# The sine half of a rotary embedding on GpSimd: two instructions of 1024 columns become four of 512

## Chip, core and metric

The kernel runs on one core of a Trainium2 chip. The metric is the device time of one execution in microseconds (us). All data are float32.

## What is computed

The reference applies one full-attention block to x (8 sequences of 512 tokens, 128 features), then six layers of windowed attention (16 heads of 64, window 32) with a gated feed-forward part, and adds both back to x. The change lies in the windowed attention, where q and k are normalised per head and then rotated:

```python
q = l2norm(q) * qs                       # (k likewise)
cos, sin = (jnp.cos(freqs), jnp.sin(freqs))
q = q * cos * scale + rotate_half(q) * sin * scale
k = k * cos * inv + rotate_half(k) * sin * inv
```

`rotate_half` swaps the two halves (32 values each) of every head and negates one of them; the sign is in the sine table.

## The kernel before

After a prologue (the full-attention block, some 290 us) the six layers run as one stream of 192 tiles n = 0..191 of 128 tokens: 6 layers, 8 sequences, 4 tiles (j = n % 4) each. The four tiles of one sequence in one layer are called a batch. Each engine has its own list of steps per tile, written out by hand in `slot(c)`, one list for each of the four values of c % 4, in which steps of several tiles are mixed (`step(c, lag, ...)` runs tile c - lag). Engines meet only through semaphores.

The steps that matter here:

- VectorE (DVE), in this order in each slot: `sumsq` of the new tile for q (L1364), `sums` of the softmax of an older tile (L1332), its reciprocal (L1337), `sumsq` for k (L1364), `probs` (L1342: Pr times rs, both in SBUF), `probs_back` (L1357, a transposition), `cos_part` of the tile before (L1378: raw times the cosine table, both in SBUF, 2048 columns), `rotated` (L1384: rot plus swp, both in SBUF), in the fourth slot `ffn_stats` (L1390, L1395), `maxes` (L1320), `less_max` (L1325), and last `normed` of the new tile (L1370: raw times rr, both in SBUF).
- GpSimd (POOL): `norms` (L1100, a maximum on 32 columns into ssm, and L1102, the power -1/2 into rr, which `normed` needs), then `sin_part` (L1112, which needs `normed` and writes swp for `rotated`). Between them lie, by slot, steps of the feed-forward part: `gated` (L1128, three in a batch), `ffn_y` (L1133), `x_between` (L1121), `ffn_rstd` (L1139, L1141).
- GpSimd's order over a batch is: norms(0), sin(0); norms(1), gated 1, sin(1), gated 0; gated 2, norms(2), ffn_y, sin(2), x_between; norms(3), ffn_rstd, sin(3). So `sin_part` of a tile is followed by norms of the next tile at once for j = 3 and j = 0, by two `gated` steps for j = 1, and by `x_between` for j = 2.
- ScalarE copies projections out of PSUM (L875, which waits for `rotated` of the tile before the last), squares them (L883), and makes the normed rows of the feed-forward part (L959, which waits for `ffn_rstd`); TensorE transposes rot (L571), and `cos_part` waits for such a transposition because it overwrites rot.

Of the kernel before, what the change touches and what calls it, by code (L numbers as in the profile page):

```python
# [7 lines left out]
ALU = mybir.AluOpType  # L8
# [6 lines left out]
HEADS, DH, W = 16, 64, 32  # L15
INNER = HEADS * DH
HID = int(D * 4 * 2 / 3)
P = 128
# [42 lines left out]
def wait(eng, sem, value):  # L61

    if type(value) is int and value <= 0:
        return
    eng.wait_ge(sem, value)


def adaln_block(nc, x_d, wq_d, wk_d, wv_d, wo_d, bq_d, bk_d, bv_d, bo_d, cT_d, wmod_d,
# [3 lines left out]
    with ctx:  # L72
        def sb(name, shape, dt=F32):
            return ctx.enter_context(nc.sbuf_tensor(name, shape, dt))
# [13 lines left out]
        TS = sb("TS", [P, DEPTH, TPB, 2, DH])  # L88
# [223 lines left out]
        def layer(n):  # L312
            return n // NT
# [741 lines left out]
        def _(pool):  # L1055
# [48 lines left out]
            def sin_part(n, b, j):  # L1104

                pool.wait_ge(qn_ready, n + 1)
                wait(pool, rot_ready, n)
                src = raw[:, j % 2, :].rearrange("p (i h t d) -> p i h t d", i=2, t=2, d=32)
                dst = swp[:, :].rearrange("p (i h t d) -> p i h t d", i=2, t=2, d=32)
                for t in range(2):  # L1110
                    tab = TS[:, layer(n), j, :, 32 * t:32 * t + 32]
                    last = pool.tensor_tensor(dst[:, :, :, t, :], src[:, :, :, 1 - t, :],  # L1112
                                              tab.unsqueeze(2).broadcast_to([P, 2, HEADS, 32]), ALU.mult)
                last.then_inc(sin_ready, 1)

            def x_between(b):
# [26 lines left out]
            def slot(c):  # L1143
                if c % TPB == 0:
                    step(c, 0, norms)
                    step(c, 0, sin_part)
                elif c % TPB == 1:
                    step(c, 0, norms)
                    batch(c, 2, gated, 1)
                    step(c, 0, sin_part)  # L1150
                    batch(c, 2, gated, 0)
                elif c % TPB == 2:
                    batch(c, 2, gated, 2)
                    step(c, 0, norms)
                    batch(c, 2, ffn_y)
                    step(c, 0, sin_part)
                    batch(c, 1, x_between)
                else:
                    step(c, 0, norms)
                    batch(c, 1, ffn_rstd)  # L1160
                    step(c, 0, sin_part)
# [322 lines left out]
```

## Time and profile before

| | |
|---|---|
| Median of 3 runs | 3816.96 us (3797.87 to 3832.17) |
| The profiled execution: its own time | 3803.09 us |
| Its span, first to last instruction | 3801.2 us |
| Mean granted TensorE clock | 0.96 |
| Busy: PE, DVE, ACT, POOL | 89%, 87%, 64%, 72% |

Busy shares are of the span. Spans are recorded by engine; a busy engine may be held up inside an instruction, and then the instruction is recorded as longer.

### The profile page before, as it was taken

What the parts mean: (1) busy time and instruction counts of PE and PEld (TensorE: products, weight loads), DVE (VectorE), ACT (ScalarE), POOL (GpSimd) and SP (SyncE); (2) the same over time, 40 slices, a digit from 0 to 9 for tenths busy, and PEclk for the clock granted to TensorE, in tenths of its full rate; (3) what the DMA queues carried; (4) which work ended last, traced back from release to release, by engine and by line L of the source; (5) the groups of instructions that cost most, each with busy time, mean ns of one, the idle gap of its engine ahead of it and who ended that gap; (6) DMA issues with size and microseconds to landing.
All of it is one profiled execution on the core that took longest, in us unless ns stands there. A gap on an engine that the chain in (4) does not pass through costs nothing.

```text
span 3801.2 us, 108012 instructions
## 1 busy us (share of the span) xinstructions
PE 3394.8 (89%) x46108; PEld 2202.2 (58%) x46108; DVE 3304.5 (87%) x2938; ACT 2421.1 (64%) x3929; POOL 2746.2 (72%) x1233
## 2 busy tenths in 40 slices
PE   4666899999999999999999999999999998999987
PEld 2333566666666665665665666665666665666654
DVE  4667899998899998899998999998999998998982
ACT  2444666666666666666766766666666666666764
POOL 3006787777787877777777787877777787787781
PEclk8778999999999999999999999999999999999997
DMA  2000111111111111111111111111111111111111
GB/s 69 3 1 14 34 38 34 38 45 45 38 39 34 38 45 44 39 38 33 34 50 44 41 36 34 39 45 44 44 34 37 34 45 46 42 34 37 35 32 40
DMA packets 132142, 141.98 MB, mean 37 GB/s; under 512 B 37580, under 2 KB 75856, under 8 KB 131664
## 3 DMA queue, kind: packets, MB, share of 16 engines
q1 hardware_dynamic: 131664, 135.09, 14.4%
q8 instruction: 364, 5.96, 0.7%
q14 instruction: 114, 0.93, 0.1%
HBM read 19.62 MB, written 2.10 MB: 6 GB/s over the span
## 4 chain that ended last, share of the span: by engine, by line
PE 37%; DVE 24%; POOL 13%; issue 11%; ACT 3%; SPq 3%; DMA 2%; POOLq 0%; ACTq 0%; DVEq 0%
PE bank L562 11%; POOL rr L1102 6%; PE mid L612 5%; DVE Pr L1342 4%; DVE raw L1370 4%; PE mid L571 4%; PE bank L660 4%; DVE rot L1378 4%; PE bank L631 4%; POOL swp L1112 3%; PE mid L599 3%; PE mid L619 2%; DVE rot L1384 2%; PE bank L668 2%; DVE ss L1364 2%
## 5 line engine op out<-in xcount | busy, mean ns | idle before, releaser
L1112 POOL TENSOR_TENSOR swp<-raw,TS 128x1024 f32<-128x1024 f32 x384 | 899.8, 2371 | 616.3 <-DVE raw L1370 616.3
L1102 POOL TENSOR_TENSOR rr<-ssm,nhalf 128x32 f32<-128x32 f32 x192 | 1213.3, 6319 | 16.0
L562 PE MATMUL bank<-wqkv,xs 128*128 128x512 f32 x2304 | 1203.5, 625 | 22.6 <-DMA xs<-F 8.5
L875 ACT ACTIVATE raw<-bank 128x512 f32<-128x512 f32 x768 | 434.3, 591 | 549.2 <-DVE rot L1384 503.3
L571 PEld LDWEIGHTS mid<-ident,rot 128*128 128x128 f32 x3072 | 365.9, 143 | 388.0 <-issue 333.6
L571 PE MATMUL mid<-ident,rot 128*128 128x128 f32 x3072 | 442.0, 277 | 136.5 <-DVE rot L1384 131.6
L562 PEld LDWEIGHTS bank<-wqkv,xs 128*128 128x128 f32 x2304 | 385.4, 192 | 289.9 <-issue 192.2
L1364 DVE TENSOR_REDUCE ss<-sq 128x16 f32<-128x1024 f32 x384 | 463.3, 1207 | 95.4 <-ACT sq L883 94.8
L1370 DVE TENSOR_TENSOR raw<-raw,rr 128x2048 f32<-128x2048 f32 x192 | 469.2, 2444 | 35.5 <-POOL rr L1102 35.5
L1378 DVE TENSOR_TENSOR rot<-raw,TC 128x2048 f32<-128x2048 f32 x192 | 440.4, 2294 | 41.7 <-PE mid L571 40.5
L1384 DVE TENSOR_TENSOR rot<-rot,swp 128x2048 f32<-128x2048 f32 x192 | 440.1, 2292 | 20.7 <-DVE rot L1378 0.9
L612 PEld LDWEIGHTS mid<-PT,V 128*64 128x64 f32 x6144 | 340.0, 138 | 191.4 <-issue 165.6
L883 ACT ACTIVATE sq<-raw 128x1024 f32<-128x1024 f32 x384 | 407.0, 1060 | 31.3 <-DVE ss L1364 25.0
L612 PE MATMUL mid<-PT,V 128*64 128x128 f32 x6144 | 383.9, 278 | 37.1 <-DMA PT<-PTd 32.8
L631 PE MATMUL bank<-OT,fwo 128*128 128x128 f32 x3072 | 383.1, 279 | 1.4 <-ACT OT L922 1.4
L631 PEld LDWEIGHTS bank<-OT,fwo 128*128 128x128 f32 x3072 | 367.6, 196 | 2.0 <-issue 2.0
L1342 DVE TENSOR_TENSOR Pr<-Pr,rs 128x1024 f32<-128x1024 f32 x192 | 359.0, 1870 | 0.1
L599 PEld LDWEIGHTS mid<-kT,qT 64*32 64x32 f32 x24576 | 273.7, 105 | 87.1 <-issue 82.5
L660 PE MATMUL bank<-xn,w 128*128 128x512 f32 (+1 forms) x576 | 313.5, 626 | 7.2 <-ACT ge L972 3.8
L599 PE MATMUL mid<-kT,qT 64*32 64x64 f32 x24576 | 309.5, 225 | 0.8 <-issue 0.8
L900 ACT ACTIVATE qT<-mid 128x512 f32<-128x512 f32 x384 | 230.1, 599 | 91.9 <-PE mid L571 88.2
L1332 DVE TENSOR_REDUCE sm<-Pr 128x16 f32<-128x1024 f32 x192 | 232.6, 1211 | 49.9 <-ACT Pr L916 49.9
(132 smaller groups left out, 4325.4 us busy)
## 6 DMA issues: line engine op xcount, KB each, us to landing
PT<-PTd SPq DMA_DIRECT2D x1344, 64.0 KB
xs<-F SPq DMA_DIRECT2D x192, 64.0 KB, 1.9
BT<-PTd SPq DMA_DIRECT2D x192, 64.0 KB
wqkv<-d_wqkv SPq DMA_DIRECT2D x36, 256.0 KB, 2.7
fwo<-d_fwo SPq DMA_DIRECT2D x6, 512.0 KB, 4.0
d_out<-X SPq DMA_DIRECT2D x8, 256.0 KB, 2.3
w<-d_w SPq DMA_DIRECT2D x6, 341.0 KB
w<-d_w SPq DMA_DIRECT2D x6, 128.0 KB
```

The costliest lines, as they stand in the source:

```text
L562: nc.tensor.matmul(bank[bk][:, :], xs[:, j, :], wqkv[:, c, :], start=True, stop=True)\
L571: mm = nc.tensor.transpose(bank[QK_BANK[i]][:, u * P:(u + 1) * P], rot[:, col:col + P], ident[:, :])
L599: mm = nc.tensor.matmul(bank[3 + h][w * W:(w + 1) * W, u * DH:(u + 1) * DH], qT[r, j % 2, u, w * W:(w + 1) * W], kT[r, u, j * P + w * W:j ...
L612: mm = nc.tensor.matmul(OUT_BANK[u // 4][h * DH:(h + 1) * DH, (u % 4) * P:(u % 4 + 1) * P], V[:, j % 2, hc:hc + DH], PT[:, :, h * HH + u, ...
L631: mm = nc.tensor.matmul(bank[6][:, j * P:(j + 1) * P], fwo[:, c, :], OT[:, c, :], start=(c == 0), stop=(c == HH - 1), skip_group_check=True)
L1102: pool.tensor_tensor(rr[:, :], ssm[:, :], nhalf[:, :], ALU.pow).then_inc(rr_ready, 1)
L1112: last = pool.tensor_tensor(dst[:, :, :, t, :], src[:, :, :, 1 - t, :], tab.unsqueeze(2).broadcast_to([P, 2, HEADS, 32]), ALU.mult)
L1342: nc.vector.tensor_tensor(pr, pr, rs[:, :].unsqueeze(2).broadcast_to([P, HEADS, DH]), ALU.mult)\
L1364: nc.vector.tensor_reduce(ss[:, s], sq[:, :].rearrange("p (h d) -> p h d", d=DH), AX.X, ALU.add).then_inc(ss_ready[i], 1)
L1370: nc.vector.tensor_tensor(q, q, rr[:, :].unsqueeze(2).broadcast_to([P, 2 * HEADS, DH]), ALU.mult)\
L1378: nc.vector.tensor_tensor(rot[:, :].rearrange("p (i h d) -> p i h d", i=2, d=DH), q, tab.unsqueeze(2).broadcast_to([P, 2, HEADS, DH]), ALU ...
L1384: nc.vector.tensor_tensor(rot[:, :], rot[:, :], swp[:, :], ALU.add).then_inc(rot_ready, 1)
```

## The change

`sin_part` runs once per tile. Before, it issued one instruction for each half t of the heads, over q and k together (2 x 16 x 32 = 1024 columns). Now the loop over q and k (i) is outside, so that there are four instructions of 16 x 32 = 512 columns. The data, the waits before the first, the signal after the last and the place in GpSimd's order are the same.

```diff
-                for t in range(2):
-                    tab = TS[:, layer(n), j, :, 32 * t:32 * t + 32]
-                    last = pool.tensor_tensor(dst[:, :, :, t, :], src[:, :, :, 1 - t, :],
-                                              tab.unsqueeze(2).broadcast_to([P, 2, HEADS, 32]), ALU.mult)
+                for i in range(2):
+                    for t in range(2):
+                        tab = TS[:, layer(n), j, i:i + 1, 32 * t:32 * t + 32]
+                        last = pool.tensor_tensor(dst[:, i, :, t, :], src[:, i, :, 1 - t, :],
+                                                  tab.broadcast_to([P, HEADS, 32]), ALU.mult)
                 last.then_inc(sin_ready, 1)
```

## Rows read from the trace of the kernel before

**Rows 1.** The page: span, part 1, and the chain's shares by engine

```profile
span 3801.2 us, 108012 instructions
PE 3394.8 (89%) x46108; PEld 2202.2 (58%) x46108; DVE 3304.5 (87%) x2938; ACT 2421.1 (64%) x3929; POOL 2746.2 (72%) x1233
PE 37%; DVE 24%; POOL 13%; issue 11%; ACT 3%; SPq 3%; DMA 2%; POOLq 0%; ACTq 0%; DVEq 0%
```

**Rows 2.** DVE's waits (us in total, times, longest), and one line's durations (ns min/median/max)

```profile
DVE raw L1370 <- POOL rr L1102: 35.5, 15, 6.1
...
L1342 DVE TENSOR_TENSOR Pr<-Pr,rs x192: 1214/1892/2336, 342.4 to 3734.5; 128x1024 f32<-128x1024 f32 x192
```

**Rows 3.** Durations of GpSimd multiplications of 1024 and of 64 columns

```profile
L1112 POOL TENSOR_TENSOR swp<-raw,TS x384: 2322/2367/3348, 305.2 to 3703.3; 128x1024 f32<-128x1024 f32 x192
...
L1067 POOL TENSOR_TENSOR TS<-xn,qks x24: 315/315/318, 12.6 to 34.9; 128x64 f32<-128x64 f32 x24
```

**Rows 4.** Timeline, tile 191 (start, us, engine, line; brackets: idle before)

```profile
3701.02 5.65 POOL L1112 TENSOR_TENSOR swp<-raw,TS 128x1024 f32<-128x1024 f32 x2 [1.50 <-DVE raw L1370]
...
3702.39 2.06 DVE L1342 TENSOR_TENSOR Pr<-Pr,rs 128x1024 f32<-128x1024 f32 x1
```

**Rows 5.** Timeline, POOL and DVE, from normed(106) to normed(107), j = 2

```profile
2190.79 3.04 DVE L1370 TENSOR_TENSOR raw<-raw,rr 128x2048 f32<-128x2048 f32 x1
...
2193.91 4.69 POOL L1112 TENSOR_TENSOR swp<-raw,TS 128x1024 f32<-128x1024 f32 x2 [2.23 <-DVE raw L1370]
...
2197.37 2.31 DVE L1342 TENSOR_TENSOR Pr<-Pr,rs 128x1024 f32<-128x1024 f32 x1
...
2198.87 1.77 POOL L1121 TENSOR_TENSOR FX<-qks,F 128x513 f32<-128x513 f32 x1 [0.26 <-ACT qks L931]
...
2200.61 0.29 POOL L1100 TENSOR_SCALAR ssm<-ss 128x32 f32<-128x32 f32 x1
...
2200.89 2.25 DVE L1378 TENSOR_TENSOR rot<-raw,TC 128x2048 f32<-128x2048 f32 x1
...
2209.03 2.28 DVE L1370 TENSOR_TENSOR raw<-raw,rr 128x2048 f32<-128x2048 f32 x1
```

**Rows 6.** The same stretch of another batch, normed(98) to normed(99), and after

```profile
2057.47 2.25 DVE L1378 TENSOR_TENSOR rot<-raw,TC 128x2048 f32<-128x2048 f32 x1
2057.49 2.38 POOL L1100 TENSOR_SCALAR ssm<-ss 128x32 f32<-128x32 f32 x1
...
2059.82 2.29 DVE L1384 TENSOR_TENSOR rot<-rot,swp 128x2048 f32<-128x2048 f32 x1
2059.96 7.47 POOL L1102 TENSOR_TENSOR rr<-ssm,nhalf 128x32 f32<-128x32 f32 x1
...
2067.46 2.29 DVE L1370 TENSOR_TENSOR raw<-raw,rr 128x2048 f32<-128x2048 f32 x1 [1.76 <-POOL rr L1102]
...
2071.00 1.14 ACT L959 ACTIVATE xn<-bank,rstd 128x128 f32<-128x128 f32 x4 [3.87 <-POOL rstd L1141]
```

**Rows 7.** Timeline, normed of tiles 97, 101 and 105 (j = 1)

```profile
2028.65 2.28 DVE L1370 TENSOR_TENSOR raw<-raw,rr 128x2048 f32<-128x2048 f32 x1
...
2102.65 2.28 DVE L1370 TENSOR_TENSOR raw<-raw,rr 128x2048 f32<-128x2048 f32 x1
...
2172.25 2.28 DVE L1370 TENSOR_TENSOR raw<-raw,rr 128x2048 f32<-128x2048 f32 x1
```

**Rows 8.** Timeline, the slots of j = 1, j = 3 and j = 0 (tiles 105, 107, 108)

```profile
2179.73 1.88 DVE L1342 TENSOR_TENSOR Pr<-Pr,rs 128x1024 f32<-128x1024 f32 x1
...
2214.85 2.33 DVE L1342 TENSOR_TENSOR Pr<-Pr,rs 128x1024 f32<-128x1024 f32 x1
2216.18 1.15 POOL L1100 TENSOR_SCALAR ssm<-ss 128x32 f32<-128x32 f32 x1
...
2225.34 2.28 DVE L1370 TENSOR_TENSOR raw<-raw,rr 128x2048 f32<-128x2048 f32 x1
...
2232.00 1.46 DVE L1342 TENSOR_TENSOR Pr<-Pr,rs 128x1024 f32<-128x1024 f32 x1
```

## The prediction

> **What bounds the kernel now.** I read the page first [rows 1]: TensorE 89% busy, VectorE 87%, GpSimd 72%, and a chain that changes engine all the time, 13% of it on GpSimd. No engine is the bound by itself, so I went to the waits. VectorE waits for GpSimd only 15 times, 35.5 us in all, each time in `normed` for rr [rows 2]. By that view GpSimd has room, and 0.3 us more per tile would cost nearly nothing. The durations say otherwise. `probs` (L1342) takes 1.21 us at least and 1.89 us in the median [rows 2]: same shape, same engine, so something holds it up inside the instruction.
>
> The timeline shows what [rows 5]. I count from the end of `normed` of the tile, 2190.79 + 3.04 = 2193.83, called 0. The sine pair runs from 0.08 to 4.77. `probs` is started at 3.54 and ends at 5.85. With its own 1.21 us it really began at 4.64, which is 0.13 before the pair ends. `x_between`, started at 5.04, ends at 6.81 and not at 6.3, since `probs` was running until 5.85. So a VectorE instruction with two SBUF inputs and a GpSimd instruction exclude each other here: the later one waits for the whole of the earlier. Those on VectorE are L1342, L1378, L1384 and L1370; the reductions and the transposition between them run beside GpSimd unhindered. The rule of the Trainium skill (SBUF — State Buffer, section "SBUF: two separate sides") is that the pair of ports which the two share is an exclusive lock, taken for a full instruction; the trace agrees.
>
> What matters then is who comes first. L1100 (ssm) is started at 6.78 and `cos_part` at 7.06: ssm gets in, rr's instruction (L1102) then waits for `cos_part`, is done at 14.6, and `normed` comes at 15.20 without waiting for it. In [rows 6] ssm is started at 2057.49, `cos_part` at 2057.47. The 0.02 us decide: ssm is held to the end of `cos_part` (2.38 us in place of 0.29), by then `rotated` is there before rr's instruction, and rr comes only 5.3 us after the end of `rotated`. `normed` waits 1.76 us for it. It doesn't end there: rstd is late too, ScalarE waits 3.87 us for it before L959, and the next slot loses more. I followed this through the 45 batches from tile 9 to tile 189. 34 went as [rows 5], 11 as [rows 6]. [rows 7] are one of each: 2028.65 to 2102.65 is 74.0 us, 2102.65 to 2172.25 is 69.6 us. Over all of them the means are 74.4 and 70.0: a batch that loses this race costs 4.4 us.
>
> **The change, part by part.** It removes 2 instructions of 1024 columns per tile and adds 4 of 512. The reads, the table values and the writes are the same in number.
>
> Length: 2.322 us for 1024 columns, 0.315 us for 64 [rows 3], so 2.09 ns per column and 0.18 us fixed, and 512 columns take 1.25 us. In a row, the pair of [rows 5] takes 4.69, 2.345 each, so a quarter takes up to 1.27. Four take 5.0 to 5.1 us in place of 4.7: 0.3 to 0.4 us per tile, some 65 us over 192 tiles, on GpSimd. Less than linear is possible too (an access pattern of one dimension fewer), but the 64-column row has that fewer and fits the line; I put the bounds at 4.6 and 5.2. For swp's reader this is nothing: `rotated` of the tile comes 4.6 us or more after the sine part in each slot that I looked at.
>
> Ends: that is the part that counts. Before, the pair has one seam, at 2.4; now the four have three, at about 1.3, 2.6 and 3.8 (instructions ending at 0.08 + 1.25 k). Does GpSimd, at a seam between two of its own instructions, let a waiting VectorE instruction in? The trace has one case [rows 4]: `probs` is started at 3702.39, inside the first sine instruction, which ends at 3701.02 + 2.32 = 3703.34; it ends at 3704.45, so it began at 3703.24, at the seam, and the pair took 5.65 instead of 4.69, as the second waited. VectorE gets in.
>
> The third slot (after `normed` of j = 2), as it will go, by these steps. `probs` is started at 3.54, in the third instruction (2.6 to 3.85), and gets in at the seam, at about 3.73. It ends at 4.94, and not at 5.85. `cos_part` comes 1.21 us later as now (5.85 to 7.06): 6.15, TensorE's transposition being ready by 6.0 in most of these slots. The fourth sine instruction starts at 4.83 and ends at 6.08. `x_between` follows at once (its input from ScalarE was there by 5.04, and no longer holds it) and takes 1.29, until 7.3; `cos_part` waits for it and runs from 7.2 to 9.4. ssm is behind `cos_part`, by over 1 us and not by 0.02. `rotated` follows, to 11.8, and rr is done 5.3 us after that, at 17.1. `normed` was at 15.2. Should `cos_part` get in before `x_between`, rr comes at about the same time or later. So the VectorE instruction that comes 0.9 us early makes the whole pattern of [rows 6] regular. The seam is met if `probs` is started before 3.7; it was 3.53 to 3.64 in nearly all of the 34 good batches. After a bad batch the next one's came at 3.54 in 8 of 11 and at 3.66 or later in 3, and those would go on as now. So about 8 in 10 batches should go the bad way, 38 of 47, against 11: 27 more, times 4.4 us is +119 us. The bounds for this term are 12 batches (+53) and all 36 (+158).
>
> The first and second slots [rows 8]: `probs` is started at 2232.00 - (2225.34 + 2.28) = 4.38 (j = 0) and at 2179.73 - (2172.25 + 2.28) = 5.2 (j = 1, counted from [rows 7], behind a `gated` step that starts when the sine part ends). Neither can use a seam; both wait for an end that is 0.3 later. TensorE bounds about half of these slots and covers it there. I take 0.35 us per batch, times 48: +17 us, bounds 0 and +28.
>
> The fourth slot (j = 3): in a bad batch `probs` comes late, at 5.5, behind the sine part, with TensorE ahead of it as the bound, and loses nothing.
>
> Sum: 3803.1 (the profiled execution's own time, 1.9 above its span) + 119 + 17 = 3939 us, +3.6%. The median of the three runs lies 0.4% above the profiled execution, so I say 3945.
>
> **The rivals.**
> (A) GpSimd keeps the lock over its own seams. The skill says that each of GpSimd's cores starts its share of the next instruction as soon as it has finished its share of the one before (GPSIMD Engine Reference, section "Instruction dispatch"); by that rule a seam need be no gap. [rows 4] speaks against it, but it is one case. Or the quarters are 5% shorter than computed and `probs` misses the seam. Then `probs` ends 0.3 later in each slot, the order of all steps stays, and 0.28 x 4 x 48 = 54 us is the most; TensorE's half of two slots hides a third of it. Against it stands a gain: in 5 of the 11 bad batches ssm lost by less than 0.2 us, and a `cos_part` that comes 0.28 later gives it back, -22 us. 3803 + 36 - 22 = 3817, up to 3840 without the gain.
> (B) The races of j = 3 and j = 0 are lost as well. For j = 3 in a good batch `probs` is started at 3.54 and ssm at 4.87 [rows 8], which runs before `cos_part` at 7.07 without trouble. After the change ssm is started at 6.17 and `cos_part` at 6.15: a toss-up, and lost it costs 2.1 us (rr at 16.1, `normed` now at 14.0). With a stall in one slot the other engines catch up, `probs` comes at 3.54 in the next, and that slot meets the same. With 2 us more per batch on top of all 36: 3803 + 158 + 17 + 2 x 36 = 4050.
> (C) Faster. The place is the third slot: if VectorE doesn't get in at the seam and all 11 bad batches turn good because `cos_part` is pushed behind ssm there, that gives 11 x 4.4 = 48 us, with the 0.3 us hidden elsewhere: 3755. It decides when `cos_part` is later by more than ssm lost by; for 3 of the 11 that was over 0.4 us, so all 11 is much to ask.
>
> **How the numbers follow.** The forecast 0.63, its own range 3860 to 3995; A 0.20; B 0.10; C 0.05; 0.02 for what I haven't thought of. About 1% (38 us) is what a measurement of this kernel can tell from no change. A lies within it for the most part, and the low end of the forecast touches it: same 0.18. C gives faster, with a little of A: 0.06. Slower 0.76. The range goes from 3815, which takes in most of A, to 4005, which leaves most of B out.
>
> **What would show it.** L1112: 768 instructions of about 1.25 us, some of them 2.4 us (with `probs` inside). L1342's median falls in the slots j = 2 while its slot gets longer. L1100 shows some 38 instructions of over 2 us in slots j = 2, where there are about 11, L1370's wait for rr grows from 35 us to 80 or more, and ACT's L959 waits for rstd in as many batches. If L1342 in the third slot ends near 6.13 and L1100 keeps its length, A was right. If L1100 is over 2 us after j = 3 or j = 0, B was. I would be wrong above all if the seam closes or is missed, or if TensorE's lateness lets `cos_part` come after ssm.

## The result and the profile after

The changed kernel takes 3977.99 us in the median of 6 runs (3974.15 to 3983.49), the kernel before 3816.73 us. The ratio is 1.0436, with a 95% interval of 1.0404 to 1.0467: slower by 4.4%, where 3.4% was forecast (3945 against 3817) in a range to 4005. The profiled executions differ by 3974.8 - 3801.2 = 173.6 us of span.

From the page of the changed kernel, against [rows 1]:

```profile
span 3974.8 us, 108204 instructions
PE 3449.1 (87%) x45916; PEld 2243.6 (56%) x46108; DVE 3328.6 (84%) x2938; ACT 2420.1 (61%) x3929; POOL 2978.0 (75%) x1617
POOL 50%; PE 18%; issue 14%; DVE 7%; ACT 3%; DMA 0%; POOLq 0%; ACTq 0%; SPq 0%; DVEq 0%
```

GpSimd's share of the chain has gone from 13% to 50%, though its busy time has only gone from 72% to 75% of the span. In the changed kernel the line numbers behind the sine part are one higher than before; the kernels of the experiments have numbers of their own. The waits of VectorE, ScalarE and TensorE in the changed kernel (total, times, longest), then ScalarE's and TensorE's in the kernel before:

```profile
DVE raw L1371 <- POOL rr L1102: 99.3, 52, 6.1
ACT xn L959 <- POOL rstd L1142: 170.4, 44, 4.2
PE bank L650 <- ACT xn L959: 195.9, 45, 4.5
```

```profile
ACT xn L959 <- POOL rstd L1141: 46.4, 12, 3.9
PE bank L650 <- ACT xn L959: 58.8, 31, 4.5
```

`normed` waited for rr 15 times [rows 2] and now waits 52 times. The late rstd that follows such a wait, seen once in [rows 6], came 12 times and now comes 44 times. TensorE in turn waits for what ScalarE makes from rstd. The total of a wait counts only what the waiting engine was idle: VectorE's and ScalarE's have grown by 64 and 124 us, and the view does not say why rr is late.

Two groups of the changed kernel, by line (ns min/median/max):

```profile
L1113 POOL TENSOR_TENSOR swp<-raw,TS x768: 1250/1279/3331, 305.6 to 3883.2; 128x512 f32<-128x512 f32 x192
```

```profile
L1343 DVE TENSOR_TENSOR Pr<-Pr,rs x192: 1215/1735/2357, 343.3 to 3910.1; 128x1024 f32<-128x1024 f32 x192
```

A quarter takes 1.25 us at least, as computed, and 1.28 in the median. The median of `probs` has gone down, from 1.89 to 1.74 us, in the slower kernel. The timeline of the changed kernel for the stretch that [rows 5] show of the kernel before, `normed` of tile 106 to `normed` of tile 107, and ScalarE behind it:

```profile
2278.18 3.37 DVE L1371 TENSOR_TENSOR raw<-raw,rr 128x2048 f32<-128x2048 f32 x1
...
2281.63 5.95 POOL L1113 TENSOR_TENSOR swp<-raw,TS 128x512 f32<-128x512 f32 x4 [2.22 <-DVE raw L1371]
...
2285.09 1.35 DVE L1343 TENSOR_TENSOR Pr<-Pr,rs 128x1024 f32<-128x1024 f32 x1
...
2287.54 1.08 POOL L1122 TENSOR_TENSOR FX<-qks,F 128x513 f32<-128x513 f32 x1
...
2287.64 3.13 DVE L1379 TENSOR_TENSOR rot<-raw,TC 128x2048 f32<-128x2048 f32 x1
...
2288.60 2.32 POOL L1100 TENSOR_SCALAR ssm<-ss 128x32 f32<-128x32 f32 x1
...
2290.88 2.29 DVE L1385 TENSOR_TENSOR rot<-rot,swp 128x2048 f32<-128x2048 f32 x1
2291.01 7.48 POOL L1102 TENSOR_TENSOR rr<-ssm,nhalf 128x32 f32<-128x32 f32 x1
...
2298.52 2.29 DVE L1371 TENSOR_TENSOR raw<-raw,rr 128x2048 f32<-128x2048 f32 x1 [1.76 <-POOL rr L1102]
...
2302.06 1.14 ACT L959 ACTIVATE xn<-bank,rstd 128x128 f32<-128x128 f32 x4 [3.87 <-POOL rstd L1142]
```

Counted from the end of `normed`, 2281.55: `probs` is started at 3.54 and done at 4.89, its own 1.21 us from 3.68 on. It is in between the third and the fourth sine instruction, and the four take 5.95 us with it. `x_between` comes at 5.99, before `cos_part` (6.09), which waits for it and ends at 9.22. ssm, started at 7.05, waits for `cos_part`; `rotated` is there 0.13 us before rr's instruction; rr is done at 16.94 and `normed` begins at 16.97, where it began at 15.20 before.

I followed the 45 batches from tile 9 to tile 189 again. I call a batch bad when `normed` of j = 3 waits for rr, as in [rows 6]. There are 42 bad ones, 11 before. They last 75.2 us in the mean (74.4 before), and the mean of all 45 is 75.0 against 71.1. That is 45 x 3.9 = 176 us, the whole difference of the spans. The stretches between two `normed` have changed so, in the mean of all 45 batches:

| from `normed` of | before | changed |
|---|---|---|
| j = 1 to j = 2 (second slot) | 18.61 us | 18.92 us |
| j = 2 to j = 3 (third) | 18.65 us | 20.04 us |
| j = 3 to j = 0 (fourth) | 17.07 us | 19.46 us |
| j = 0 to j = 1 (first) | 16.75 us | 16.58 us |

So more of the loss arises behind the late rr, in the fourth slot (2.4 us per batch), than where rr is waited for (1.4 us). One thing there stands in no part of the prediction. TensorE waits 4.5 us, until 2303.35, for what L959 writes, and in this wait the clock granted to it falls; before it, from 2290.8 to 2300.8, it was busy for 6.49 of 10 us. The first instruction behind the wait, and the activity from 2300.8 to 2307.6 (length of the stretch, busy time of PE, PEld, DVE, ACT and POOL, granted clock, DMA):

```profile
2303.35 1.09 PE L650 MATMUL bank<-ident,xn 128*128 128x128 f32 x4 [4.50 <-ACT xn L959]
```

```profile
2300.80:2307.60 6.80, 4.25 (x14) 3.15 (x15) 4.96 (x6) 3.63 (x9) 6.63 (x7) 0.50 0.03 9
```

A granted clock of 0.50 is the lower of TensorE's two levels, 1.2 GHz. During this wait or just behind it every bad batch has it, in both kernels: before for 3.4 us in 8 of them and 6.8 us in 3, in the changed kernel for 3.4 us in 4 and 6.8 us in 38. Of the 34 good batches before, 27 have no such time, and 7 have 3.4 us of it. The fourth slot of a bad batch lasts 19.0 us with 3.4 us at the lower level and 20.0 with 6.8 before, 19.1 and 19.6 in the changed kernel. No run here holds the clock fixed, so how much of a bad batch's cost is the clock, and how much the wait itself, stays open.

### The profile page after: what moved, and what is told of

Same layout as the page of the kernel before. It is cut to its first block, busy times and chain, and to the rows that moved or that the text cites. A ratio compares the mean times of both kernels' runs of the same rounds, so it can differ in the third digit from the quotient of the medians.

```text
span 3974.8 us, 108204 instructions
## 1 busy us (share of the span) xinstructions
PE 3449.1 (87%) x45916; PEld 2243.6 (56%) x46108; DVE 3328.6 (84%) x2938; ACT 2420.1 (61%) x3929; POOL 2978.0 (75%) x1617
## 4 chain that ended last, share of the span: by engine, by line
POOL 50%; PE 18%; issue 14%; DVE 7%; ACT 3%; DMA 0%; POOLq 0%; ACTq 0%; SPq 0%; DVEq 0%
POOL rr L1102 20%; POOL swp L1113 16%; PE bank L562 6%; POOL ssm L1100 4%; POOL ge L1129 3%; PE mid L571 3%; DVE rot L1379 3%; DVE rot L1385 3%; PE bank L631 3%; POOL vpe L1140 3%; PE mid L612 3%; PE mid L619 1%; POOL F L1134 1%; POOL FX L1122 1%; PE bank L650 1%
## 5 line engine op out<-in xcount | busy, mean ns | idle before, releaser
L1113 POOL TENSOR_TENSOR swp<-raw,TS 128x512 f32<-128x512 f32 x768 | 1005.7, 1348 | 598.8 <-DVE raw L1371 598.8
L562 PE MATMUL bank<-wqkv,xs 128*128 128x512 f32 x2304 | 1221.2, 633 | 26.9 <-ACT V L889 11.3
L1102 POOL TENSOR_TENSOR rr<-ssm,nhalf 128x32 f32<-128x32 f32 x192 | 1229.8, 6405 | 16.0
L571 PEld LDWEIGHTS mid<-ident,rot 128*128 128x128 f32 x3072 | 377.7, 146 | 378.3 <-issue 330.1
L571 PE MATMUL mid<-ident,rot 128*128 128x128 f32 x3072 | 456.3, 283 | 107.5 <-DVE rot L1385 102.6
L1379 DVE TENSOR_TENSOR rot<-raw,TC 128x2048 f32<-128x2048 f32 x192 | 473.8, 2467 | 88.5 <-PE mid L571 87.8
L631 PE MATMUL bank<-OT,fwo 128*128 128x128 f32 x3072 | 397.0, 285 | 1.4 <-ACT OT L922 1.4
L631 PEld LDWEIGHTS bank<-OT,fwo 128*128 128x128 f32 x3072 | 385.0, 204 | 1.9 <-issue 1.9
L1343 DVE TENSOR_TENSOR Pr<-Pr,rs 128x1024 f32<-128x1024 f32 x192 | 335.4, 1747 | 0.1
L1321 DVE TENSOR_REDUCE mx<-mid 128x16 f32<-128x1024 f32 x192 | 233.3, 1215 | 48.4 <-PE mid L599 47.2
```

The lines of the kernel that those rows point to most:

```text
L562: nc.tensor.matmul(bank[bk][:, :], xs[:, j, :], wqkv[:, c, :], start=True, stop=True)\
L571: mm = nc.tensor.transpose(bank[QK_BANK[i]][:, u * P:(u + 1) * P], rot[:, col:col + P], ident[:, :])
L631: mm = nc.tensor.matmul(bank[6][:, j * P:(j + 1) * P], fwo[:, c, :], OT[:, c, :], start=(c == 0), stop=(c == HH - 1), skip_group_check=True)
L1102: pool.tensor_tensor(rr[:, :], ssm[:, :], nhalf[:, :], ALU.pow).then_inc(rr_ready, 1)
L1113: last = pool.tensor_tensor(dst[:, i, :, t, :], src[:, i, :, 1 - t, :], tab.broadcast_to([P, HEADS, 32]), ALU.mult)
L1379: nc.vector.tensor_tensor(rot[:, :].rearrange("p (i h d) -> p i h d", i=2, d=DH), q, tab.unsqueeze(2).broadcast_to([P, 2, HEADS, DH]), ALU ...
```

## The experiments

Ratios are to the kernel before, run together with it, with 95% intervals. The runs come in three groups, each with its own runs of the kernel before (medians 3809, 3803 and 3814 us); the three sine variants of the first experiment and the changed kernel without the clamp are of the first, the kernel before without the clamp and the clamp on VectorE of the second, the rest of the third. "Bad" batches are counted as above, of 45, each time in one profiled execution. The kernel before ranges from 3788 to 3843 us in the 19 runs of the first group, so a count alone may differ by some from run to run.

**Where the seams lie: three instructions in two orders, and one instruction.** The cut shows both orders, one loop line for each kernel.

```diff
-                for t in range(2):
-                    tab = TS[:, layer(n), j, :, 32 * t:32 * t + 32]
-                    last = pool.tensor_tensor(dst[:, :, :, t, :], src[:, :, :, 1 - t, :],
-                                              tab.unsqueeze(2).broadcast_to([P, 2, HEADS, 32]), ALU.mult)
+                for t, h0, h1 in ((0, 0, HEADS), (1, 0, 10), (1, 10, HEADS)):    # seam late
+                for t, h0, h1 in ((0, 0, 6), (0, 6, HEADS), (1, 0, HEADS)):      # seam early
+                    tab = TS[:, layer(n), j, :, 32 * t:32 * t + 32]
+                    last = pool.tensor_tensor(dst[:, :, h0:h1, t, :], src[:, :, h0:h1, 1 - t, :],
+                                              tab.unsqueeze(2).broadcast_to([P, 2, h1 - h0, 32]), ALU.mult)
```

and, for one instruction:

```diff
+                tab = TS[:, layer(n), j, :, :].rearrange("p i (t d) -> p i t d", t=2)
+                last = pool.tensor_tensor(dst, src[:, :, :, ::-1, :],
+                                          tab.unsqueeze(2).broadcast_to([P, 2, HEADS, 2, 32]), ALU.mult)
```

> The sine part in three instructions of 1024, 640 and 384 columns: the last seam lies at about 3.8 us after the end of normed, behind the start of probs in the third slot (3.54). Seam theory: probs gets in there, ends at 5.0, ssm is overtaken as in the changed kernel, in nearly all batches (over 35 of 45): ratio to before 1.035 to 1.045. Length theory (the time is that of the added fixed cost per instruction, and GpSimd is on the chain): one instruction more in place of two more, so half of the change's loss, 1.02, and the same as the mirrored order.

> The same three sizes in the order 384, 640, 1024: seams at 1.0 and 2.45 us, then one instruction until 4.8, so that probs (3.54) waits for its end as before. Seam theory: ratio 1.00 to 1.01, about 11 of 45 batches with ssm held up, as before. Length theory: 1.02, as the order 1024, 640, 384.

> The sine part in one instruction of 2048 columns (the half swap by a reversed dimension). Seam theory: before has no seam that probs meets (its one seam is at 2.4), so only 0.1 to 0.2 us per tile shorter: ratio 0.99 to 1.00. Length theory: one instruction less in place of two more, so half of the change's loss gained, 0.98. If a pattern with four dimensions is slower per column on GpSimd, the instruction is over 4.7 us and the ratio above 1.

Seam late: 3975.52 us, ratio 1.040 (1.0347 to 1.0454), 42 bad batches. Seam early: 3807.15 us, ratio 0.998 (0.9952 to 1.001), 7 bad batches. The two kernels issue the same three sizes. VectorE's waits for rr, in the first and in the second:

```profile
DVE raw L1370 <- POOL rr L1102: 94.3, 51, 6.1
```

```profile
DVE raw L1370 <- POOL rr L1102: 28.5, 11, 6.1
```

The order of 1024, 640 and 384 columns costs 4%, the order 384, 640, 1024 nothing. Neither the number of instructions nor the work that GpSimd has with them tells the two apart. That the place of the last seam makes the loss is shown by this pair.

One instruction: 3830.47 us, ratio 1.004 (1.000 to 1.008). The seam theory had 0.99 to 1.00, so it missed by a little, although the instruction itself is shorter than the pair's 4.69 us:

```profile
L1111 POOL TENSOR_TENSOR swp<-raw,TS x192: 4509/4552/4577, 306.1 to 3727.0; 128x2048 f32<-128x2048 f32 x192
```

The profiled execution has 17 bad batches in place of 11. The sine part ends 0.14 us earlier, and in the good batches `cos_part` is started 0.11 us earlier too, while `x_between` still waits for ScalarE (`L931`, 48 times) and starts at the same time. By this reading `cos_part` wins the race more often, the same mechanism by another way. It is argued, not shown: the two kernels' runs overlap (3810 to 3863 us against 3788 to 3843), and the difference of 21 us is no more than five bad batches.

**The change for one tile of the batch alone.** The new loop stands under `if j == 2:` or `if j == 3:`, the old one under `else:`.

> The kernel before with the four instructions of 512 for j = 2 alone, two of 1024 for the other three tiles of a batch. Seam theory: the loss is made in the third slot, so nearly all of it is here: ratio 1.035 to 1.045, ssm over 2 us in over 38 of 45 slots j = 2. Length theory: a quarter of the loss, 1.01.

> The kernel before with the four instructions of 512 for j = 3 alone. The third slot stays as before (about 11 of 45 batches go badly). What is left is the toss-up of rival B: cos_part at 6.15 against ssm at 6.17. If ssm loses it (rr at 16.1 in place of 14.0 in some 34 slots): 34 x 2.1 = 71 us, ratio 1.02. If it wins: 1.00. Length theory: 1.01.

j = 2 alone: 3958.33 us, ratio 1.038 (1.0349 to 1.0405), 39 bad batches. The third slot holds seven eighths of the loss. j = 3 alone: 3843.42 us, ratio 1.008 (1.0047 to 1.0106), between the two values expected, with 15 bad third slots. The timeline of that kernel from the slots of tile 103 and of tile 115:

```profile
2157.48 1.39 DVE L1349 TENSOR_TENSOR Pr<-Pr,rs 128x1024 f32<-128x1024 f32 x1
...
2160.08 2.25 DVE L1385 TENSOR_TENSOR rot<-raw,TC 128x2048 f32<-128x2048 f32 x1
2160.10 2.39 POOL L1100 TENSOR_SCALAR ssm<-ss 128x32 f32<-128x32 f32 x1
...
2170.07 2.29 DVE L1377 TENSOR_TENSOR raw<-raw,rr 128x2048 f32<-128x2048 f32 x1 [2.77 <-POOL rr L1102]
...
2372.58 1.36 DVE L1349 TENSOR_TENSOR Pr<-Pr,rs 128x1024 f32<-128x1024 f32 x1
...
2375.16 0.30 POOL L1100 TENSOR_SCALAR ssm<-ss 128x32 f32<-128x32 f32 x1
2375.17 2.35 DVE L1385 TENSOR_TENSOR rot<-raw,TC 128x2048 f32<-128x2048 f32 x1
...
2382.86 2.29 DVE L1377 TENSOR_TENSOR raw<-raw,rr 128x2048 f32<-128x2048 f32 x1 [0.41 <-POOL rr L1102]
```

In the first `cos_part` is started 0.02 us before ssm, and `normed` comes at 16.13 us after the end of the last one; in the second ssm is started 0.01 us before, and `normed` comes at 13.82. In 23 of the 45 slots `probs` got in at a seam; the first pattern followed in 18 of them, the second in 5. In the other 22 `probs` came too late for a seam. So rival B is real where the third slot goes well. In the changed kernel it had hardly a place, since after a bad third slot `probs` is started at 5.5.

**One GpSimd instruction fewer in `norms`.** If rr is late because two instructions of GpSimd, ssm and the power, are each overtaken by one of VectorE, then with one instruction there is only one wait.

```diff
-                pool.tensor_scalar(ssm[:, :], ss[:, :], 1e-24, None, ALU.max).then_inc(ssm_ready, 1)
-                pool.wait_ge(ssm_ready, n + 1)
-                pool.tensor_tensor(rr[:, :], ssm[:, :], nhalf[:, :], ALU.pow).then_inc(rr_ready, 1)
+                pool.tensor_tensor(rr[:, :], ss[:, :], nhalf[:, :], ALU.pow).then_inc(rr_ready, 1)
```

`sumsq` waits for rr_ready in place of ssm_ready. Both of these kernels leave the clamp out.

> The changed kernel with norms in one GpSimd instruction: the clamp of the sums at 1e-24 (L1100) is left out, and the power reads ss itself. Seam theory, with its second half (ssm is held by cos_part, and only for that reason rr by rotated too): the power now waits for cos_part alone, rr is ready at 14.7 in the third slot, before normed (15.3), and nearly the whole loss goes: ratio to before 0.99 to 1.01. Rival (any instruction on GpSimd costs its own time, some 0.4 us per tile): 1.03 to 1.035.

> The kernel before with norms in one GpSimd instruction (the clamp at 1e-24 left out). The 11 batches in which ssm is overtaken have no ssm left, so no stall for rr: at least 11 x 4.4 = 48 us less, ratio 0.985. What is left of the difference to the changed kernel without the clamp (0.968) is what the seams give when nothing is overtaken: probs ends at 4.9 in place of 5.85 in slots j = 2 and j = 3, up to 0.9 us each, 1.8 per batch, 86 us or 2.3%. Theory that the seams are a gain by themselves: this kernel at 0.98 to 0.99, slower than the changed one without the clamp. Rival (the clamp is worth the same in both and the seams are worth nothing): 0.965 to 0.97.

The changed kernel without the clamp: 3697.18 us, ratio 0.968 (0.9617 to 0.9735), below the 0.99 to 1.01 that was expected. The kernel before without it: 3717.69 us, ratio 0.977 (0.9743 to 0.9798), between the two theories' values. No batch between tile 9 and tile 189 has a wait for rr in either. An instruction of 0.3 us of its own, taken from an engine that is idle a quarter of the time, is worth 2.3% in the kernel before and 7% in the changed one (3697.18 / 3977.99 = 0.929, from different groups). The change is turned from a loss of 4.4% into a gain of 0.5 to 1% (20.5 us by the medians, 1% by the ratios, from different groups).

More than the missing bad batches is in it: 11 x 4.4 = 48 us, while the batches of the kernel before have become 45 x 1.6 = 72 us shorter. Without ssm the power comes before `cos_part` in the second slot already and is done at 13.6 us and not at 15.9. So `ffn_y` (L1133 before) is over when `normed` of j = 2 comes, and this takes 2.28 us, where it is held and takes 3.11 in the good batches of the kernel before.

Of the seams, I had expected up to 2.3%, on the ground that two slots per batch meet them. Only the fourth does: it lasts 15.65 us in the one kernel and 16.32 in the other. In the third slot `probs` is started at 4.0 in the mean in both now, mostly too late for the seam (41 of 45 in the changed kernel without the clamp).

**The clamp on VectorE, whole kernels.** L1100 is removed with the waits in front of it, and behind `probs` VectorE does it (its call in each slot is not shown):

```diff
+            def clamp(n, b, j):
+                for i in range(2):
+                    dve.wait_ge(ss_ready[i], n + 1)
+                wait(dve, qn_ready, n)
+                nc.vector.tensor_scalar(ssm[:, :], ss[:, :], 1e-24, None, ALU.max).then_inc(ssm_ready, 1)
```

> The kernel before, nothing left out: the clamp of the sums is made on VectorE behind probs (one more instruction of 32 columns there, some 0.15 us per tile, 29 us if all of it counts), and GpSimd's norms is the power alone. Gain as without the clamp (48 us or more) less that: ratio 0.985 to 1.00. If VectorE's time is what counts in most slots: 1.00.

> The changed kernel, nothing left out, with the clamp on VectorE behind probs. As the changed kernel without the clamp (0.968) plus up to 0.15 us per tile: ratio to before 0.97 to 0.98, faster than both kernels. If the clamp, now behind probs and in VectorE's order, holds the power longer than GpSimd's own did: above 0.985.

On the kernel before: 3748.96 us, ratio 0.985 (0.9824 to 0.9884). On the changed kernel: 3760.17 us, ratio 0.989 (0.9852 to 0.9919), which missed 0.97 to 0.98 and is not the faster of the two. The new instruction by line, in the first and in the second kernel:

```profile
L1367 DVE TENSOR_SCALAR ssm<-ss x192: 167/170/1253, 299.4 to 3630.5; 128x32 f32<-128x32 f32 x192
```

```profile
L1368 DVE TENSOR_SCALAR ssm<-ss x192: 167/178/1256, 298.2 to 3646.5; 128x32 f32<-128x32 f32 x192
```

It takes 0.17 us or 1.25 us, and the total of the group is 83.0 us in the first and 132.7 us in the second. In both kernels it takes some 1.2 us in the second slot (j = 1), in the second kernel in the fourth slot too: there `probs` gets in at the seam and ends at 4.9, the last sine instruction follows, and the clamp waits for all of it, and with it what VectorE does next. `cos_part` is started at 7.15 us, where it comes at 6.25 in the fourth slot of the changed kernel without a clamp instruction. The seam's gain is given back at once. This is read from the traces; no run moves the clamp to test it.

**The clamp inside `normed`, whole kernels, and the best of each.** The power reads ss itself, as above, and its result is clamped, as a minimum with 1e12, in the instruction that multiplies anyway:

```diff
-                nc.vector.tensor_tensor(q, q, rr[:, :].unsqueeze(2).broadcast_to([P, 2 * HEADS, DH]), ALU.mult)\
+                nc.vector.scalar_tensor_tensor(out=q, in0=rr[:, :].unsqueeze(2).broadcast_to([P, 2 * HEADS, DH]),
+                                               scalar=1e12, in1=q, op0=ALU.min, op1=ALU.mult)\
```

The second kernel has besides the four instructions for j = 3 and the one instruction for j = 0, 1 and 2.

> The changed kernel with nothing left out: the power reads ss itself, and the clamp is made as a minimum with 1e12 inside normed (one VectorE instruction with two operations, in place of the multiplication). As the changed kernel without the clamp, ratio 0.968, if the two operations cost no time; if they cost 0.1 us per tile, 0.973. If L1100 had cost by its own length and not by being overtaken, nothing changes against the changed kernel without the clamp either; this run is for a version that is whole.

> As the run with the minimum in normed, but the sine part in four instructions for j = 3 alone, where probs meets the seam, and in one of 2048 columns (4.55 us in place of 5.0) for j = 0, 1, 2, where probs waits for the end of the sine part. Seam theory: the seam of j = 3 is kept (probs ends at 4.9), and the three other slots get an end that is 0.4 us earlier, of which TensorE hides a half or more: ratio 0.955 to 0.967. If seams at any place are a gain: above 0.97.

The first: 3695.51 us, ratio 0.969 (0.9665 to 0.9716). The second: 3678.94 us, ratio 0.965 (0.9622 to 0.9671); its four runs (3673.70 to 3682.14) all lie below those of the first (3689.25 to 3701.38). It is 3.5% faster than the kernel before and 7.5% faster than the changed one (3678.94 / 3977.99 = 0.925, from different groups). The fourth slot of the first of them, from `normed` of tile 107 on:

```profile
2143.85 2.28 DVE L1369 SCALAR_TENSOR_TENSOR raw<-rr,raw 128x2048 f32<-128x2048 f32 x1
...
2149.67 1.39 DVE L1341 TENSOR_TENSOR Pr<-Pr,rs 128x1024 f32<-128x1024 f32 x1
...
2152.14 5.43 POOL L1100 TENSOR_TENSOR rr<-ss,nhalf 128x32 f32<-128x32 f32 x1
2152.26 2.28 DVE L1378 TENSOR_TENSOR rot<-raw,TC 128x2048 f32<-128x2048 f32 x1
...
2159.30 2.28 DVE L1369 SCALAR_TENSOR_TENSOR raw<-rr,raw 128x2048 f32<-128x2048 f32 x1
```

`normed` takes 2.28 us with two operations, as it does with one where nothing holds it. `probs` gets in at the seam, the power starts 0.12 us before `cos_part` and is done in 5.43 us, and the slot lasts 15.45 us from `normed` to `normed`, where [rows 5] and [rows 8] give 16.31 (2209.03 to 2225.34).

## Why the prediction was right

**That the two engines exclude each other inside instructions, and that VectorE gets in at a seam** rested on one case, tile 191 [rows 4]. In the third slots of the changed kernel `probs` gets in whenever it is started by 3.75 us, 41 times of 45, and in none of the 4 where it is started at 3.77 or later; the two orders of the same three instructions show that the seam decides. Rival A, the lock kept over the seam, is excluded by these runs. The rule of the Trainium skill that was weighed there as a reason for it (GPSIMD Engine Reference, section "Instruction dispatch"), that each core starts its share of the next instruction once it has finished its share of the one before, may still be so: no run here shows the single cores. It closes no seam here.

**One sentence of the prediction was too wide**: that each of the two engines waits for the whole of the other's instruction. It holds in the rows for the sine part, `x_between` and ssm, and not for the power. The power waits for the end of a VectorE instruction that came first, but once it runs, VectorE's two-input instructions run beside it: `cos_part` takes its usual 2.28 us from 0.12 us behind the power's start in the rows of the last experiment, and in [rows 6] nothing but `rotated`, which came first, makes 7.47 us of a power of 5.43. The steps of the forecast used it rightly.

**The course of the third slot** was forecast as 4.94, 6.15, 9.4 and 17.1 us for the ends of `probs`, the start and end of `cos_part` and the end of rr. It was 4.89, 6.09, 9.22 and 16.94. The time in between is smaller as `x_between` took 1.08 us and not 1.29.

**How many batches** was put too low: 27 more bad ones of 47 forecast, from the late `probs` of 3 in 11 next batches. It was 31 more of 45. A batch in which `probs` comes too late for the seam has become rare: the third slot's `probs` is started at 3.58 in the mean. 31 x 4.4 = 135 us, against +119.

**The first and second slots** were put at 0.35 us per batch, bounds 0 and 0.58. Over all 45 batches they have become 0.13 us longer together (+0.30 and -0.17 in the table above), inside the bounds and less than half of what was put down: some 6 us in place of 17.

**What a bad batch costs** was the term that was mis-sized most. It was taken over from the kernel before at 4.4 us, the difference between its bad and its good batches, but a bad batch of the changed kernel is 0.8 us longer than a bad one before. 0.54 us of it lie in the third slot: `normed` of j = 2, which opens it, takes 3.12 us, held by `ffn_y` as in the good batches before, and 2.43 in the bad ones before. 0.29 us lie in the fourth, from 19.29 to 19.58 us, which the prediction had as "loses nothing": wrong. The sine part of the fourth slot starts at 1.2, behind rstd, and ends at 6.13 in place of 5.84, and `probs`, started at 5.5 in both kernels, waits for it in both. The time at the lower clock is longer there too, as shown above, and the two are not told apart. The sum: 31 x 4.4 = 135, 42 x 0.8 = 33, and 7 us in the three good batches, is the 176 us.

**Two smaller slips.** In the kernel before ssm lost by less than 0.2 us in 8 of the 11 bad batches and not in 5, so rival A's gain was -35 us by its own reasoning and not -22. And the median lies 0.4% above the profiled execution, which makes 3953 of the sum of 3939; 3945 has less than half of it.

**Rival B** had its toss-up right (lost in 18 of the 23 slots where it occurred) and its place in the changed kernel wrong: I let the slot behind a stall meet a seam too, and there `probs` is late. **Rival C** may have occurred in small, in the seam early kernel with 7 bad batches in place of 11, but its 0.998 (to 1.001) can't be told from no change.

Not tested: how much of a bad batch's cost is the wait for rr, how much the late rstd behind it, and how much TensorE's lower clock behind that. From a good batch before to a bad one in the changed kernel, the third slot gains 1.9 us and the fourth 3.2.

## What to carry to other kernels

Where VectorE and GpSimd work side by side, look at the minimum and the median of VectorE's two-input instructions: here the gap (1.21 and 1.89 us for `probs`) was time in which GpSimd held it, and ssm's 0.29 and 2.4 us are the other way round. Then the ends of GpSimd's instructions decide the order in which the two take turns, and cutting one into pieces can let the wrong instruction in; ask of each seam who will be waiting there, and what that one overtakes next. A chain of two small instructions on the engine that can be overtaken is worth making one, though they are short: here the 0.3 us of a clamp were worth 2.3% in one kernel and 7% in the other. And when a stall of one engine has passed on to TensorE, look at its granted clock behind the stall.

## What the runs showed of the hardware that I had not expected

- A one-input instruction of VectorE on 32 columns in SBUF (the clamp on VectorE) is held by GpSimd like the two-input ones: it takes up to 1.25 us, and 0.17 us alone. The reductions next to it (`sumsq`, 1.16 to 1.22 us) and the transposition (1.23 to 1.25 us) never were.
- GpSimd's power on 32 columns takes 5.43 us alone and does not hold VectorE's two-input instructions while it runs: of those started at least 0.02 us after it in the first kernel with the clamp in `normed`, all 147 `cos_part` took 2.25 to 2.35 us.
- A GpSimd multiplication over four dimensions, one of them reversed, takes 4.55 us for 2048 columns, 2.22 ns per column, less than two of 1024 (4.69).
- The race between `cos_part` and ssm is decided by 0.01 to 0.02 us. The same kernel has therefore batches of 70 and of 74 us. That 0.1 us anywhere before the race changes how many there are of each is likely by this, and not shown.
- TensorE's granted clock falls to 0.50 during or just behind its wait for L959 in a bad batch (4.5 us in the rows above), and stays there for 3.4 or 6.8 us.
- A minimum and a multiplication in one VectorE instruction take the time of the multiplication (2.28 us for 2048 columns).
